# One place per state tile in a ring of twelve SBUF tiles for a selective scan: decay, state and weighted state share it

## The reference

```python
def step(hst, inp):
    u_i, dt_i, b_i, c_i = inp
    dA = jnp.exp(dt_i[..., None] * A)
    hst = dA * hst + (dt_i * u_i)[..., None] * b_i[:, :, None, :]
    y = jnp.einsum('bkdn,bkn->bkd', hst, c_i)
    return (hst, y)
_, ys = lax.scan(step, h0, (u_t, dt_t, b_t, c_t))
return ys.transpose(1, 2, 3, 0) + D[None, :, :, None] * u
```

## Time and profile before

| | us |
|---|---|
| median of 3 runs (13094.11 to 13113.85) | 13094.34 |
| the profiled execution's own time | 13113.0 |
| its span | 13111.2 |
| from the first scan to the end of DVE's and POOL's last work of the scan stage | about 10677 |

### The profile page before, as it was taken

How to read it: one execution, slowest core, us unless ns; L and a number is a source line. 1 busy time by engine, 2 the same in 40 slices (tenths; PEclk the granted TensorE clock), 3 DMA queues, 4 the chain that set the end, 5 groups by cost and what they waited for, 6 DMA issues and landing times. The chain is left out here.

```text
span 13111.2 us, 148286 instructions
## 1 busy us (share of the span) xinstructions
PE 9546.4 (73%) x34584; PEld 3395.6 (26%) x34584; DVE 10558.8 (81%) x6847; ACT 9124.6 (70%) x15557; POOL 9200.7 (70%) x3956
## 2 busy tenths in 40 slices
PE   8867676677777777766777776777767676669888
PEld 2322222222222222222222222222222222223333
DVE  6768888888888888888888888888888888866665
ACT  6767777777777777777777777777777777735555
POOL 0038888888888888888888888888888888822111
PEclk9977877778787877787878787888777888879998
DMA  3456666666666666666666666666666666644442
GB/s 101 127 138 159 158 161 160 163 160 159 153 159 163 161 156 160 158 162 160 163 156 161 159 155 163 161 160 157 159 161 160 163 163 163 160 109 104 102 101 52
DMA packets 577621, 1948.60 MB, mean 149 GB/s; under 512 B 106614, under 2 KB 111638, under 8 KB 562198
## 3 DMA queue, kind: packets, MB, share of 16 engines
q1 hardware_dynamic: 573714, 1938.65, 61.8%
q10 hardware_dynamic: 3076, 0.97, 0.0%
HBM read 1532.38 MB, written 406.85 MB: 148 GB/s over the span
## 5 line engine op out<-in xcount | busy, mean ns | idle before, releaser
L1057 POOL TENSOR_TENSOR dBu<-rep,shared 128x1024 f32<-128x1024 f32 x2304 | 5366.8, 2353 | 972.4 <-DMA rep<-dd_dram 866.6
L747 PE MATMUL py<-hC,fold 128*32 128x512 f32 x12288 | 2599.6, 766 | 1450.9 <-ACT y L917 1258.6
L1016 DVE TENSOR_TENSOR_SCAN pd<-pd,dBu 128x1024 f32<-128x1024 f32 x1536 | 3506.1, 2283 | 165.5 <-ACT dBu L851 138.7
L826 ACT ACTIVATE pd<-rep,a_now 128x1024 f32<-128x1024 f32 x2304 | 2560.9, 1112 | 354.4 <-DVE hC L1025 167.8
L1067 POOL TENSOR_TENSOR hC<-shared 128x1024 f32<-128x1024 f32 x768 | 1797.1, 2360 | 816.0 <-DVE shared L997 814.8
L1067 POOL TENSOR_TENSOR hC<-h,shared 128x1024 f32<-128x1024 f32 x768 | 1804.5, 2350 | 797.2 <-DVE h L1016 794.4
L1025 DVE TENSOR_TENSOR hC<-pd,shared 128x1024 f32<-128x1024 f32 x1536 | 1880.5, 1224 | 395.0 <-PE py L747 249.0
L1016 DVE TENSOR_TENSOR_SCAN h<-pd,dBu 128x1024 f32<-128x1024 f32 x768 | 1751.4, 2280 | 71.0 <-ACT dBu L851 49.1
L997 DVE TENSOR_TENSOR_SCAN shared<-shared,carry,pd 128x1024 f32<-128x1024 f32 x576 | 1319.2, 2330 | 522.9 <-PE pd L727 408.1
L883 ACT ACTIVATE shared<-shared,turned_b 128x192 f32<-128x192 f32 x4096 | 1551.7, 442 | 0.0
L747 PEld LDWEIGHTS py<-hC,fold 128*32 128x32 f32 x12288 | 493.9, 129 | 3262.0 <-issue 2957.0
(11 more groups left out here) (170 smaller groups left out, 12357.4 us busy)
## 6 DMA issues: line engine op xcount, KB each, us to landing
rep<-dd_dram SPq DMA_DIRECT2D x1024, 768.0 KB, 12.1
shared<-bc_dram SPq DMA_DIRECT2D x3584, 128.0 KB, 3.9
u<-u_dram SPq DMA_DIRECT2D x128, 768.0 KB, 5.8
dd_dram<-LG SPq DMA_DIRECT2D x256, 384.0 KB, 3.5
dd_dram<-RL SPq DMA_DIRECT2D x256, 384.0 KB, 3.7
y_dram<-y SPq DMA_DIRECT2D x256, 384.0 KB, 3.7
shared<-y_dram SPq DMA_DIRECT2D x63, 1536.0 KB, 16.0
u_dram<-shared SPq DMA_DIRECT2D x32, 1536.0 KB, 7.6
```

The costliest lines, as they stand in the source:

```text
L747: last = mm(py[32 * g:32 * g + 32, t2(t)], fold[:, :], hC[:, j % 2 * 3 + g, t2(t)], start=(j % 4 == 0), stop=(j % 4 == 3), skip_group_chec ...
L826: go(dst, rep[:, half, 0, g, :], ACT.Exp, scale=a_now[:, column(i)]).then_inc(S.exped, 1)
L1016: v.tensor_tensor_scan(turned(dst, k), turned(pd[:, i % 2, :], k), turned(dBu[:, ring(c, place(i)), :], k), 0.0, ALU.mult, ALU.add).then_i ...
L1057: nc.gpsimd.tensor_tensor(dBu[:, ring(c, p), :], rep[:, half, 1, g, :], BB[:, r, :], ALU.mult).then_inc(S.dbu, 1)
```

## The change

Every tile gets one place for dA, state and weighted state. There are twelve such places (`RING`): nine are in a tensor `h`, three in the shared region; tile i uses place i % 12. `expo` writes dA there, the scan works in place there, both `weigh`s multiply in place there, and `reduce_states` reads there. `pd` in PSUM then holds the drives of turned tiles alone. The tensors `hs` and `hC` and one of the two `y` tiles are gone.

`fold_state` is gone; every scan of c > 0 takes `carry[:, i:i+1]` as its start value. A `weigh` waits for `save_state` of its tile, since it overwrites the state. `expo` runs three tiles ahead and waits for the `reduced` of the triple four before. DVE scans a whole triple and then weighs its first two tiles. PE, ACT's `STEPS`/`SCALE` tables and the place of `make_step`, `turn_b`, `copy_b`, `skip` and `add_up` are laid out anew. POOL's order of instructions is as before.

```diff
+        RING = 12
-        hs = a.shared[:, 9 * T:12 * T].rearrange("p (g t) -> p g t", g=3)
-        CC = a.shared[:, 12 * T:16 * T].rearrange("p (r t) -> p r t", r=4)
+        CC = a.shared[:, 9 * T:13 * T].rearrange("p (r t) -> p r t", r=4)
+        h_shared = a.shared[:, 13 * T:16 * T].rearrange("p (i t) -> p i t", i=3)
-        h = sb("h", [128, 2, T])
-        hC = sb("hC", [128, 6, T])
+        h_own = sb("h", [128, RING - 3, T])
-        y = sb("y", [HALF, 2, T])
+        y = sb("y", [HALF, T])
+        def state(i):
+
+            slot = i % RING
+            return h_own[:, slot, :] if slot < RING - 3 else h_shared[:, slot - RING + 3, :]
...
+            def turn_back(n, i):
+                if i - 9 < 2:
+                    pe.wait_ge(S.scanned, done(scanned(n - 1, i + 4)))
                 else:
                     pe.wait_ge(S.scanned, done(scanned(n, i - 2)))
...
+                act.wait_ge(S.reduced, done(n * 8 + i // 3 - 3))
+                go(state(i), rep[:, half, 0, g, :], ACT.Exp, scale=a_now[:, column(i)]).then_inc(S.exped, 1)
             def save_state(bk, k, c, i):
+                act.wait_ge(S.scanned, done(scanned(bk * NC + c, i)))
+                go(carry[:, i:i + 1], state_column(i, last_of(k)), ACT.Identity).then_inc(S.carried, 1)
-            def fold_state(bk, k, c, i):
...
             def scan(bk, k, c, i):
+                n = bk * NC + c
+                dve.wait_ge(S.exped, done(scanned(n, i)))
+                if is_turned(i):
+                    dve.wait_ge(S.dbu_turned, done(n * TURNED + i - 8))
+                    drive = pd[:, i % 2, :]
+                else:
+                    dve.wait_ge(S.dbu, done(driven(n, place(i))))
+                    drive = dBu[:, ring(c, place(i)), :]
+                first = 0.0
+                if c > 0:
+                    dve.wait_ge(S.carried, done(carries(bk, c - 1, i)))
+                    first = carry[:, i:i + 1]
+                v.tensor_tensor_scan(turned(state(i), k), turned(state(i), k), turned(drive, k),
+                                     first, ALU.mult, ALU.add).then_inc(S.scanned, 1)
+
+            def weigh(bk, c, i):
                 dve.wait_ge(S.scanned, done(scanned(n, i)))
+                if i < 12:
+                    dve.wait_ge(c_loaded[r], done((n + 1) * 64))
+                if c < NC - 1:
+                    dve.wait_ge(S.carried, done(carries(bk, c, i)))
+                v.tensor_tensor(state(i), state(i), CC[:, r, :], ALU.mult).then_inc(S.hc_dve, 1)
...
+                for j in range(8):
+                    for i in range(3 * j, 3 * j + 3):
+                        scan(bk, k, c, i)
+                        if left and i in (10, 20):
+                            delta_u(n + 1, 1 - s, (10, 20).index(i))
+                    if not is_turned(3 * j):
+                        weigh(bk, c, 3 * j)
+                        weigh(bk, c, 3 * j + 1)
```

More of the change, by code:

```diff
@@ L599, in store_y @@
                 sp.sem_inc(S.passed, 1)
-                sp.dma_start(a.y_flat[row, :, half, :], y[:, half, :]).then_inc(y_stored[half], 16)
+                sp.dma_start(a.y_flat[row, :, half, :], y[:, :]).then_inc(y_stored, 16)
             def load_first_y(n):
@@ L605, in load_first_y @@
                 sp.wait_ge(S.dbu_turned, done((n + 1) * TURNED))
-                for half in range(2):
-                    sp.wait_ge(y_stored[half], done(16 * K * NC))
+                sp.wait_ge(y_stored, done(32 * K * NC))
                 for k, sem in ((0, S.y_loaded0), (1, S.y_loaded1)):
@@ L660, in _ @@
             chunk_loop(sp, body)
-            for half in range(2):
-                sp.wait_ge(y_stored[half], done(16 * BK * NC))
+            sp.wait_ge(y_stored, done(32 * BK * NC))
         @block.tensor
@@ L726, in turn_back @@
                         pe.wait_ge(S.scaled, done(n * SCALED + min(J * q + 7, SCALED)))
+                    half, r, g = where(i)
                     last = nc.tensor.transpose(pd[:, i % 2, block_of(q)], turned_dbu[:, q, half * 3 + g, :, :],
@@ L810, in expo @@
                     act.wait_ge(rep_loaded[half], done((n + 1) * 64))
-                before, q = at(n, i - 2)
-                if r == 3:
-                    before, q = at(n, 9 + g if half else 12 + g - NS)
-                    act.wait_ge(S.hc_pool, done(weighed_pool(before, q)))
-                    if half and c < NC - 1:
-                        act.wait_ge(S.carried, done(carries(bk, c, q)))
-                    elif not half and c > 0:
-                        act.wait_ge(S.carried, done(carries(bk, c - 1, q)))
-                    dst = hs[:, g, :]
-                else:
-                    if where(q)[1] < 3 and where(q)[2] < 2:
-                        act.wait_ge(S.hc_dve, done(weighed_dve(before, q)))
-                    else:
-                        act.wait_ge(S.scanned, done(scanned(before, q)))
-                    dst = pd[:, i % 2, :]
@@ L844, in fold_state @@
-            def fold_state(bk, k, c, i):
-                n = bk * NC + c
-                slot = ring(c, place(i))
-                act.wait_ge(S.exped, done(scanned(n, i)))
-                act.wait_ge(S.dbu, done(driven(n, place(i))))
-                act.wait_ge(S.carried, done(carries(bk, c - 1, i)))
-                go(dBu[:, slot, first_of(k)], pd[:, i % 2, first_of(k)], ACT.Identity, scale=carry[:, i:i + 1],
-                   bias=dBu[:, slot, first_of(k)]).then_inc(S.folded, 1)
+                act.wait_ge(S.reduced, done(n * 8 + i // 3 - 3))
@@ L1016, in scan @@
-                v.tensor_tensor_scan(turned(dst, k), turned(pd[:, i % 2, :], k),
-                                     turned(dBu[:, ring(c, place(i)), :], k),
-                                     0.0, ALU.mult, ALU.add).then_inc(S.scanned, 1)
-            def weigh(n, i):
-                half, r, g = where(i)
-                dve.wait_ge(S.scanned, done(scanned(n, i)))
-                dve.wait_ge(c_loaded[r], done((n + 1) * 64))
-                dve.wait_ge(S.reduced, done(n * 8 + i // 3 - 1))
-                v.tensor_tensor(hC[:, i % 6, :], pd[:, i % 2, :], CC[:, r, :], ALU.mult).then_inc(S.hc_dve, 1)
+                dve.wait_ge(S.scanned, done(scanned(n, i)))
@@ L1034, in body @@
                 n, s = bk * NC + c, c % 2
-                for i in range(NS):
-                    scan(bk, k, c, i)
-                    if not is_turned(i) and i % 3 < 2:
-                        weigh(n, i)
-                    if i == 9 and left:
-                        delta_u(n + 1, 1 - s, 0)
-                    if i == 19 and left:
-                        delta_u(n + 1, 1 - s, 1)
+                for j in range(8):
[6 more added lines that the diff above has]
+                        weigh(bk, c, 3 * j + 1)
             chunk_loop(dve, body)
```

152 lines of the change are left out of this document (56 added, 96 removed).

## The result

| | before | after |
|---|---|---|
| median, us | 13099.01 (13094.11 to 13113.85, 4 runs) | 18003.11 (17999.66 to 18013.46, 4 runs) |
| span of the profiled execution, us | 13111.2 | 18001.7 |
| scan stage, first scan to last work, per chunk | 83.4 us | 121.7 us |

The ratio is 1.3743, 95% interval 1.3719 to 1.3766: slower by 37%. The prediction was 17,970 us in a range of 17,000 to 19,400.

A forecast was written before the change was run, and what follows sets the result against it. VectorE and GpSimd, near full side by side, would take turns at SBUF: 36.5 (scans) + 11.3 (weighs) + 70.5 (GpSimd) + 3 idle, rounded 121.5 us a chunk against 83.4, times 128 is 4877 more; 17,970 us, range 17,000 to 19,400.

The forecast's parts named there:

- The mechanism: Scan stage: VectorE instructions with two SBUF inputs and GpSimd instructions reading SBUF take turns; forecast 4877 us more in all.
- The size of a turn: Scan stage: an instruction holds GpSimd up by its length less 0.28 us, 2.03 for a scan, 0.94 for a weigh.
- a scan behaves as L1676 does: Unturned scans: inferred to take turns like the last stage's two-SBUF-input L1676, whose 0.742 us held GpSimd up by 0.46.
- rival 1: Scan stage: scans take no turns, only instructions such as the weigh; 89 us a chunk, 13,810 us; chance 0.08.
- The chunk: Scan stage: 118.3 us of turns plus 3 idle, 121.3 rounded to 121.5 us, in place of 83.4.
- That last term: Turned tiles: 3 us a chunk in which nobody has the turn, about 17 us less 14 filled by GpSimd's weighs.
- a window of 17 us for the turned tiles: Turned tiles: 13.9 + 1.2 us plus about 2 of stalls, as tile 14's transposes still stand behind make_step.
- each of these weighs must wait for its scan: Turned tiles: GpSimd's six weighs, 14.1 us, run beside the turned scans, each only after its own scan.
- save_state, priced at zero: Weigh's new wait for ScalarE's save_state: zero; if cover were gone, 1 to 2 us at one or two triples a chunk.
- fold_state and the pointer: ScalarE loses fold_state, 4.7 us a chunk, with waits of 2.2: hidden, worth nothing; a pointer scan takes 2.323 against 2.286.
- The signs named: Profile after: unturned scans near 4 us, drives near 3.9, TensorE at half and ScalarE too, chunk of 119 to 124 us.
- GpSimd "over 90%": Profile after: VectorE and GpSimd both over 90% busy in the scan stage.

The follow-up runs named there:

- pool_writes_only: The kernel after with each of GpSimd's 30 products of a chunk replaced by a memset of the same tile; 12,091 us in one run.
- decay_in_psum: The kernel after with dA of unturned tiles in PSUM, expo two tiles ahead, scans still writing state to SBUF; 13,337 us in one run.
- before_order: The kernel before with two moves on TensorE alone (skip and make_step behind transposes of turned tiles), fold_state kept; 12,787 us, ratio 0.9764.
- before_pointer_order: The kernel before with carry by pointer, no fold_state, and skip and make_step moved behind transposes on TensorE; 12,621 us, ratio 0.9634.

## Why the prediction was right

- **The mechanism.** Turns between VectorE's two-input instructions and GpSimd's products: read from the earlier trace rows for 512 elements and an instruction that is no scan. pool_writes_only and decay_in_psum each take one side of the meeting away, and the long rows of the scans go. So semaphores are not the only place where these engines meet: the two also hold each other up at SBUF.
- **The size of a turn.** Forecast: a scan holds GpSimd up by 2.03 us, a weigh by 0.94. Measured: 4.32 - 2.35 = 1.97 and 3.32 - 2.35 = 0.97. The inference that a scan behaves as L1676 does held; rival 1 falls by the 4.37 us of the scans.
- **The chunk.** 121.5 us forecast (121.3 before rounding), 121.7 measured. Two small errors cancel: with the measured 1.97 and 0.97 the turns are 18 x 1.97 + 12 x 0.97 + 30 x 2.35 = 117.6 in place of 118.3, which leaves 4.1 us where I had 3. That last term was near in size and wrong in make-up, so its nearness is luck. I had a window of 17 us for the turned tiles, stretched by late transposes, of which GpSimd's six weighs fill 14. VectorE waited for the transposes by 0.7 us in the whole kernel, and the window (start of scan 9 to end of scan 14) was 14.7 us in the median. But GpSimd stood idle in it. Its wait in front of these weighs, in the kernel after, by what ended it:

```profile
  ACT carry L818: 483.8, 289
  DVE shared L972: 146.3, 64
```

  That is (483.8 + 146.3) / 128 = 4.9 us a chunk. The profile puts most of it down to ScalarE's save_state, since that came last, but save_state was waiting too. The scan of tile 9, ScalarE's save behind it, and GpSimd's weigh behind that:

```profile
6006.46 2.33 DVE L972 TENSOR_TENSOR_SCAN shared<-shared,carry,pd 128x1024 f32<-128x1024 f32 x1
6008.83 0.20 ACT L818 ACTIVATE carry<-shared 128x1 f32<-128x1 f32 x1 [6.51 <-DVE shared L972]
6009.11 4.70 POOL L1026 TENSOR_TENSOR shared<-shared 128x1024 f32<-128x1024 f32 x2 [3.65 <-ACT carry L818]
```

  The scan ends at 6008.79 and the save starts 0.04 us later, so of GpSimd's 3.65 us 3.3 are the scan's. Each weigh paired with its scan in the trace: of the 4.9 us, 4.0 pass before the scan has ended (3.3 at tile 9 and 0.6 at tile 11, which stands behind delta_u), and 0.9 behind it, 0.7 of them with save_state's start and length. So the prediction's sentence that each of these weighs must wait for its scan was right, but the wait for the first scan was missing from its window, and save_state, priced at zero, cost under 1 us. The last two weighs then run into the first in-place scans: in this chunk they end at 6026.64, 5.5 us behind scan 14.
- **fold_state and the pointer.** Priced at nothing. No run has the kernel after with fold_state; for it speaks that VectorE hardly waits there and ScalarE is at 47%. On the kernel before the pointer alone was worth nothing (0.9997). It is not nothing in general, as before_order against before_pointer_order shows.
- **The signs named.** In-place scans near 4 us in the mean: 3.9. Drives near 3.9: 4.04. TensorE and ScalarE at about half: 54% and 46% of the middle. GpSimd "over 90%": 89%. Besides the 4.9 us above, its drives wait (848.9 + 283.1) / 128 = 8.8 us a chunk for the scan four tiles earlier; VectorE has the turn meanwhile, so that costs nothing.
- **The rule of the Trainium skill.** "SBUF — State Buffer", section "Who interferes with whom", names the meeting, its condition (GpSimd reads) and its exception (GpSimd only writes); pool_writes_only agrees with the last at 0.95 us memsets. The same page of the Trainium skill, section "SBUF: two separate sides", has whoever starts first keep the shared pair for its whole instruction. For products of two tensors that is near: GpSimd's 2.35 us hold a scan up by 2.05, and a scan's 2.32 hold GpSimd up by 1.97. For a copy or a multiplication by a constant on GpSimd it is not: 0.73 us in both, of 1.04 and 2.76.

## What to carry to other kernels

Before an operand is moved from PSUM to SBUF to save space or to work in place, count for each VectorE instruction how many tensor inputs will lie in SBUF, and look at what GpSimd reads at that time. Where both are busy with products of two tensors, the cost is nearly the sum of the two engines' times and not the larger one, and it doesn't show as idle time: both engines look nearly full, with rows longer than the same instruction elsewhere in the trace. A spread of an instruction's length within one line, as 742 to 2726 ns in the earlier trace rows, is worth following into the timeline before the change and not after; and a stall that one edit removes is worth only what the next one, here the transposes, lets through.

## What the runs showed of the hardware

- A scan or a product on VectorE with both inputs in SBUF is as fast as with one in PSUM (2.33 and 2.32 us for scans; 1.21 and 1.22 for products) as long as GpSimd reads nothing.
- GpSimd holds a VectorE scan with two inputs in SBUF up by 2.05 us with a product of two tensors (2.35 us alone), by 0.73 with a copy (1.04 alone) and by 0.73 with a multiplication by a constant (2.76 alone); with a memset (0.95) by nothing. The other way round, a scan holds a product on GpSimd up by 1.97 us and a VectorE product does by 0.97.
- Turns alternated one by one in the kernel after (drives at 4.3 us, never over 4.37), but in the kernel with copies one copy waited 12.5 us behind seven instructions of VectorE, and in decay_in_psum a VectorE weigh took 8.0 us beside three products of GpSimd.
- On GpSimd a multiplication by a constant took longer (2.76 us) than a product of two tensors (2.35) of the same 128 x 1024.
